# The tile loop of an attention and expert kernel, rewritten with fourfold k weights and later routing tables

## The chip, the cores and the metric

The kernel runs on one core of a Trainium2 chip. The metric is the device time of one execution in microseconds; the median of 3 runs stands for a kernel. One execution is profiled, and its records are what the rows below show.

## What is computed

The reference, cut to what matters: a row-wise attention over an image, a memory layer over the tokens, and 32 experts of which each token takes two.

```python
# x: (4, 256, 32, 32); wq, wk: (32, 256); wv: (256, 256)
q = einsum('bchw,oc->bohw', x, wq) + bq
k = einsum('bchw,oc->bohw', x, wk) + bk
v = einsum('bchw,oc->bohw', x, wv) + bv
energy = einsum('bci,bcj->bij', qf, kf).reshape(b, h, w, h, w)
attn = softmax(energy, axis=-1)
out = einsum('bchk,bhwkv->bcwv', v, attn)
x = gamma * out + x
t = to_tokens(x)                                   # 4096 tokens of 256
u = layer_norm(t)
t = t + u @ W1 + (memory @ u) @ W2 + bias          # memory: a band of 32
xt = layer_norm(t)
sel_val, sel_idx = top_k(sigmoid(xt @ expert_sel.T), 2)
h = relu(einsum('td,edh->teh', xt, keys))          # 32 experts, hidden size 64
t = t + einsum('teh,te,ehv->tv', h, w, values)     # w: sel_val at sel_idx
```

## The kernel before

The 4096 tokens are 32 tiles (NT) of 128, eight for each of the 4 images (TB). The kernel is written engine by engine: each engine has its own program in a fixed order, and semaphores tie them together. An instruction that waits holds all that stands behind it on its engine. There are two parts: the tile loop, and after it the experts, which gather the tokens sorted by expert. The change touches the first.

The tile loop is a pipeline of steps `s`. In step s each engine works on several tiles, each at another stage; the lags are named at the top: attention product S_AV = 1 step behind, turn of u S_TURN = 2, mix S_MIX = 3, memory and second norm S_NORM2 = 4, routing S_ROUTE = 5, positions S_POS = 6, sending S_SEND = 7. The stages of a tile are:

- energies (TensorE, L1112): 16 matmuls of 32 x 32 with 256 columns, in two of the array's four row groups, into `E` (two banks). VectorE takes the maximum `gmax` (L755), subtracts it (L759), ScalarE takes the exponential (L638), VectorE sums (L803) and inverts (L818), GpSimd scales by it (L496, `scale_by_sums`).
- the attention product (L1207) into `av_p`; VectorE adds the input: `t1` (L829), takes statistics with BATCH_NORM_STATS and an aggregate (L835, L838); GpSimd makes the factors of the norm in three instructions (`layer_norm_factors`, L470 to L474: add epsilon, power of -1/2, times the mean); ScalarE normalises (L617).
- `u` is turned (L1218), split into a high and a low part by ScalarE (L652) and VectorE (L845), mixed with W1 and W2 (L1147), the second half again split into `z_hi` and `z_lo` (L623, L751), and the memory band is applied (L1180). VectorE adds `t1b` and takes the statistics (L769 to L778), GpSimd makes the factors (`second_factors`), ScalarE normalises into `rows` (L657, and a second copy, L645).
- the rows are turned (L1167), the logits computed (L1188), ScalarE and VectorE make sigmoid and top two (L634, L781 to L813). TensorE counts the positions in the experts' lists (L1133, L1134); VectorE makes of them the row numbers `slot` (L774 to L795) in step s = t + S_POS; GpSimd sends both rows of each token to their slots in memory with two indirect DMAs (`scatter_rows`, L478) in step s = t + S_SEND, after `rows_complete` (L489), which waits for `slot` and for the columns that ScalarE writes (L660 to L664).

Beside these, in the first 24 steps, one v projection for the next image runs in each step (L1088, evacuated by VectorE, L734), and in the steps j = 5 and 6 of eight (QK_STEPS) a projection of q and k together over 512 columns (L1067), of which ScalarE evacuates q (L605) and VectorE k (L726).

The order of GpSimd's step is: first factors (s-2), bias (s-3), `rows_complete` and scatter r=0 (s-7), second factors (s-4), scatter r=1 (s-7), scale by sums (s). TensorE's is: energies (s), turn of the rows (s-5), v projection, memory (s-4), logits (s-5), positions (s-6), attention product (s-1), turn of u (s-2), mix (s-3). After step 31 a drain finishes the last tiles, VectorE plans the experts' lists, and the experts' part begins.

## Time and profile before

| | |
|---|---|
| median of 3 runs | 504.51 us (502.11 to 505.92) |
| profiled execution | 505.35 us |
| span of its profile, first to last instruction | 503.6 us |
| mean granted clock of TensorE | 0.908 |
| tile loop, from the first to the last `gmax` | 13.8 to 276.5 us |
| first group of the experts' weights copied | about 320 us |

In the rows times are microseconds from the span's start. A timeline row has start, length, engine, line, operation, what it writes and reads, and the number of instructions merged; in brackets the idle time of the engine before it and what ended it. "issue" is time in which the engine waited for nothing that the profile shows.

### The profile page before, as it was taken

The numbers are of one execution on the slowest core, as the hardware profiler recorded it, in microseconds if no ns is written. First come the engines' busy times: TensorE is split into PE (matmuls) and PEld (weight loads), VectorE is DVE, ScalarE is ACT, GpSimd is POOL, SyncE is SP. The second block draws the span as 40 slices with busy tenths as digits, with TensorE's granted clock in tenths as the row PEclk, the third lists the DMA queues.
The fourth block names the chain that finished last, engine by engine and source line by source line (L and its number), as shares of the span: only waits on it lengthen the run. The fifth ranks groups of instructions, "written<-read, shape, count | busy, mean of one in ns | idle before, by whom it ended". The sixth has DMA issues, their size and how long they took to land.

```text
span 503.6 us, 10097 instructions
## 1 busy us (share of the span) xinstructions
PE 403.9 (80%) x2919; PEld 307.1 (61%) x2919; DVE 375.3 (75%) x1100; ACT 229.8 (46%) x604; POOL 323.6 (64%) x481
## 2 busy tenths in 40 slices
PE   8899999999999999999999875768876484876000
PEld 4667777878778786777676753356554374765000
DVE  2888999999999999999999857566655576577100
ACT  2223454545455554554554443258665474753000
POOL 5355558888778888678888786365555555536610
PEclk9999999999999999999999987699788788888555
DMA  6998001311111111112111011476544343421096
GB/s 221 318 212 170 24 23 55 127 54 45 44 43 43 54 44 55 45 38 49 55 58 40 22 53 64 127 238 190 177 148 128 126 144 106 126 85 51 1 208 126
DMA packets 28439, 49.52 MB, mean 98 GB/s; under 512 B 6204, under 2 KB 21966, under 8 KB 27373
## 3 DMA queue, kind: packets, MB, share of 16 engines
q1 hardware_dynamic: 20512, 26.69, 20.5%
q0 software_dynamic: 7872, 22.19, 14.2%
q8 instruction: 24, 0.39, 0.3%
q14 instruction: 31, 0.25, 0.2%
HBM read 30.74 MB, written 25.73 MB: 112 GB/s over the span
## 4 chain that ended last, share of the span: by engine, by line
PE 46%; DVE 18%; issue 13%; SPq 9%; DMA 3%; another core or an unknown queue 2%; POOL 2%; DVEq 1%; ACT 1%; POOLq 0%; ACTq 0%
PE bank L1207 16%; SPq L402 7%; PE bank L1147 6%; PE E L1112 5%; PE bank L1088 4%; DVE gmax L755 2%; PE bank L1180 2%; PE bank L1067 2%; DVE gsum L803 2%; PE bank L1188 2%; PE bank L1278 2%; DMA biasb<-bias 2%; PE bank L1167 2%; PE bank L1264 1%
## 5 line engine op out<-in xcount | busy, mean ns | idle before, releaser
L578 POOL DMA_INDIRECT out<-vT,dest x80 | 79.0, 988 | 65.2 <-DVE vT L1021 44.5
L1207 PE MATMUL bank<-vT,prob 128*128 128x256 f32 x512 | 118.1, 384 | 0.2 <-POOL prob L496 0.2
L1207 PEld LDWEIGHTS bank<-vT,prob 128*128 128x128 f32 x512 | 94.9, 190 | 12.4 <-POOL prob L496 0.6
L496 POOL TENSOR_TENSOR prob<-prob,ginv 128x1024 f32<-128x1024 f32 x32 | 61.1, 1909 | 28.1 <-DVE ginv L818 25.7
L478 POOL DMA_INDIRECT slot_rows<-rows,slot x64 | 68.5, 1070 | 12.7 <-issue 12.7
L1247 PE MATMUL E<-ident,xc_or_xin 128*128 128x128 f32 x160 | 26.8, 320 | 30.0 <-DMA xc_or_xin<-slot_rows 27.0
L675 ACT ACTIVATE prob<-E 128x512 f32<-128x512 f32 x40 | 22.5, 594 | 47.8 <-PE E L1247 31.8
L1247 PEld LDWEIGHTS E<-ident,xc_or_xin 128*128 128x128 f32 x160 | 20.8, 163 | 38.0 <-DMA xc_or_xin<-slot_rows 32.5
L638 ACT ACTIVATE prob<-prob 128x1024 f32<-128x1024 f32 x32 | 33.8, 1057 | 20.9 <-DVE prob L759 20.9
L1021 DVE SCALAR_TENSOR_TENSOR vT<-bank,wgt,vT 128x256 f32<-128x256 f32 x80 | 33.2, 478 | 11.9 <-PE bank L1278 8.1
L803 DVE TENSOR_REDUCE gsum<-prob 128x32 f32<-128x1024 f32 x32 | 38.5, 1204 | 4.1 <-ACT prob L638 4.0
L682 ACT ACTIVATE vT<-xc_or_xin 128x256 f32<-128x256 f32 x80 | 41.2, 588 | 0.0
L1035 DVE COPY rows<-values_s 64x256 f32 x112 | 37.5, 335 | 3.9 <-issue 2.6
L755 DVE TENSOR_REDUCE gmax<-E 128x32 f32<-128x1024 f32 x32 | 39.0, 1220 | 1.7 <-PE E L1112 1.3
L759 DVE TENSOR_TENSOR prob<-E,gmax 128x1024 f32<-128x1024 f32 x32 | 39.2, 1225 | 1.1
L472 POOL TENSOR_TENSOR rstd<-rstd,half_neg 128x1 f32<-128x1 f32 x64 | 36.5, 571 | 5.3
L652 ACT ACTIVATE uT_hi<-bank 128x256 fp32r<-128x256 f32 x32 | 12.3, 385 | 54.2 <-PE bank L1218 54.2
L617 ACT ACTIVATE u<-t,rstd 128x256 f32<-128x256 f32 x32 | 19.2, 601 | 36.3 <-POOL rstd L474 36.1
L1112 PE MATMUL E<-k_s,q_s 32*32 32x256 f32 x1024 | 35.0, 380 | 0.4 <-DVE prob L759 0.4
L1088 PE MATMUL bank<-wv,xc_or_xin 128*128 128x256 f32 x128 | 32.6, 384 | 2.2 <-issue 1.3
L470 POOL TENSOR_SCALAR rstd<-mv 128x1 f32<-128x1 f32 x64 | 14.9, 233 | 24.4 <-DVE mv L778 19.3
L697 ACT ACTIVATE k_s<-keys_s 128x128 f32 x112 | 24.7, 298 | 11.9 <-issue 11.9
(206 smaller groups left out, 888.8 us busy)
## 6 DMA issues: line engine op xcount, KB each, us to landing
xc_or_xin<-slot_rows SPq DMA_DIRECT2D x48, 130.0 KB
xc_or_xin<-slot_rows SPq DMA_DIRECT2D x64, 65.0 KB
xt<-x_tok SPq DMA_DIRECT2D x32, 128.0 KB, 2.4
values_s<-values SPq DMA_DIRECT2D x2, 2048.0 KB, 30.5
out<-out POOLq DMA_DIRECT2D x4, 1024.0 KB, 14.3
xc_or_xin<-x_cm SPq DMA_DIRECT2D x3, 1024.0 KB, 10.4
keys_s<-keys SPq DMA_DIRECT2D x1, 2048.0 KB, 15.3
out<-vT,dest POOLq DMA_INDIRECT x80
```

The costliest lines, as they stand in the source:

```text
L478: g.indirect_dma_start(out=slots_d, out_offset=bass.IndirectOffsetOnAxis(ap=slot[:, t % RB, r:r + 1], axis=0), in_=rows[:, t % RB, r, :], ...
L496: g.tensor_tensor(prob[:, t % 2], prob[:, t % 2], ginv[:, t % 2].unsqueeze(2).to_broadcast([P, WT * KB, W]), ALU.mult).then_inc(prob_done, 1)
L578: g.indirect_dma_start(out=out, out_offset=bass.IndirectOffsetOnAxis(ap=dest[:, n % (2 * NB), k:k + 1], axis=0), in_=yb[:, n % NB, k, :], ...
L682: done = a.activation(yb[:, n % NB, k, :], xin[:, n % NB, k, 0:C], ACT.Identity, bias=xin[:, n % NB, k, MEAN:MEAN + 1], scale=xin[:, n % N ...
L755: v.tensor_reduce(gmax[:, t % 2], E[:, :].rearrange("p (a v) -> p a v", v=W), AX.X, ALU.max).then_inc(max_done, 1)
L759: v.tensor_tensor(prob[:, t % 2].rearrange("p (j w) v -> p w j v", w=WT), E[:, :].rearrange("p (w j v) -> p w j v", w=WT, v=W), gmax[:, t ...
L803: v.tensor_reduce(gsum[:, t % 2], prob[:, t % 2], AX.X, ALU.add).then_inc(sum_done, 1)
L1035: done = v.tensor_copy(into, values_s[side, bass.ds(expert[2 * k + r], 1), :].rearrange("p e n -> p (e n)"))
L1088: mm = m.matmul(v_bank(b, j)[:, 0:C], x, w, start=(i == 0), stop=(i == len(terms) - 1))
L1112: mm = m.matmul(E[g * H:(g + 1) * H, cols], q_s[at, b % 2, tb, w, :], k_s[at, b % 2, g].rearrange("p j v -> p (j v)"), start=True, stop=True)
L1207: mm = m.matmul(av_p, pr[:, j, :], vT[:, b % 2, j, :], start=(j == 0), stop=(j == KB - 1))
L1247: mm = m.transpose(T_p[q][:, k % 2, a, :], xin[:, n % NB, k, a * P:(a + 1) * P], ident[:, :])
```

## The change

TensorE:

- the energies are spread over all four row groups. k is therefore made four times, once in each group of 32 partitions: its weights stand fourfold in `wqk`, and q is made by eight small matmuls into four column groups (`q_proj`, in step j = 2), k in four pieces of 256 columns (`k_proj`, steps j = 3 to 6). `E` takes the lower half of each of four banks; what else is in PSUM moves to their upper halves and to banks 4 to 7.
- the order of the step is now: turn of the rows (s-5), energies (s), memory (s-4), logits (s-5), attention product (s-1), positions (s-6), q or k projection, mix (s-3), v projection, turn of u (s-2). The v projection waits for the `t1` sum of the same step, since both are in bank 7.

VectorE:

- the statistics go. The sums `t1` and `t2` are scalar_tensor_tensor instructions with an accumulated output (`first_sum`, `second_sum`); ScalarE takes the sum of squares (`squared`: a Square with accumulated output and a tiny activation that scales it and adds epsilon). GpSimd's factors are two instructions, the fourth one of the second norm is gone.
- the routing tables come a step later: `hot` and `hotb` in step t + S_POS, positions read, `picked` and `slot` in step t + S_SEND, all behind the subtraction of the maximum.
- k is evacuated by ScalarE (`k_evac`).

GpSimd: in steps below 31 both scatters stand behind one another, ahead of the second factors, and `scale_by_sums` is last. ScalarE: new order, below.

The diff, cut to its core:

```diff
-QK_STEPS = (5, 6)
+Q_STEP, K_STEPS = 2, (3, 4, 5, 6)
...
+        X = ps("X", [P, 2048])
+        bank = [X[:, i * 512:(i + 1) * 512] for i in range(4)] + [ps(f"bank{i}", [P, 512])[:, :] for i in range(4, 8)]
+
+        E = X.rearrange("p (w c) -> p w c", w=WT)[:, :, 0:KB * W]
+        hz_p = bank[4]
         t2_p = bank[5][:, 0:C].rearrange("p (a n) -> p a n", a=CH)
-        lg_p = bank[6][:, 0:NE]
-        pos_p = bank[5][:, C:C + NE]
-
-        first_qk_p = [E[:, 0:512], bank[7]]
-        v_banks = [2, 3, 4, 5, 6, 7]
-        LAST_QK = 5
-        BEFORE_E, BEFORE_MAX, BEFORE_SUM, BEFORE_E1 = 2, 2, 4, 6
-        cnt_p = bank[3][:, 0:NE]
-        sched_p = bank[2][0:4, 0:P]
-
-        T_p = [E[:, q * 512:(q + 1) * 512].rearrange("p (k a n) -> p k a n", k=2, a=CH) for q in range(2)]
-
-        H_two = [bank[2 + b][:, :].rearrange("p (w k n) -> p w k n", w=GROUP // 2, k=2) for b in range(2)]
-        H_half = [bank[2 + b][:, :].rearrange("p (k n) -> p k n", k=GROUP) for b in range(2)]
-        Y_p = [[bank[i + side][:, :].rearrange("p (k n) -> p k n", k=GROUP // 2) for side in range(2)] for i in (6, 4)]
+        lg_p = bank[5][:, C + NE:C + 2 * NE]
+        uT_p = bank[6][:, 0:C].rearrange("p (a n) -> p a n", a=CH)
+        qk_p = bank[6][:, C:2 * C]
+        av_p = bank[7][:, 0:C]
+        v_p = bank[7][:, C:2 * C]
+
+        first_k_p, first_q_p = [bank[4], bank[5]], bank[6][:, 0:TB * H]
+        first_v_p = [bank[i][:, C:2 * C] for i in (7, 4, 5, 6)]
+        BEFORE_E, BEFORE_MAX, BEFORE_SUM, BEFORE_E1 = 1, 1, 3, 5
...
                 for t in tiles(s, S_SEND):
                     rows_complete(t)
                     scatter_rows(t, 0)
+                    if s < NT - 1:
+                        scatter_rows(t, 1)
                 for t in tiles(s, S_NORM2):
                     second_factors(t)
+                scale_by_sums(s)
                 if s == NT - 1:
-                    scale_by_sums(s)
-                for t in tiles(s, S_SEND):
-                    scatter_rows(t, 1)
-                if s < NT - 1:
-                    scale_by_sums(s)
+                    scatter_rows(s - S_SEND, 1)
                 if s == 0:
...
+            def k_evac(b, u):
+                act.wait_ge(k_mm, k_made(b - 1) + u + 1)
+                after(act, e_mm, TB * (b - 1))
+                vs = W // len(K_STEPS)
+                a.activation(k_s[:, b % 2, :, :, u * vs:(u + 1) * vs], qk_p.rearrange("p (v j g) -> p g j v", g=WT, j=KB),
+                             ACT.Identity, bias=bqk[:, 0:1]).then_inc(k_out, 1)
...
+            def squared(x, mv_t, rstd_t, t, x_done, rstd_done, mv_done, ve_done):
+
+                act.wait_ge(x_done, t + 1)
+                after(act, ve_done, t)
+                a.activation(squares[:, :], x, ACT.Square, bias=mv_t[:, 0:1], scale=-float(C),
+                             accum_out=mv_t[:, 1:2]).then_inc(mv_done, 1)
+                act.wait_ge(mv_done, t + 1)
+                after(act, rstd_done, t - 1)
+                a.activation(rstd_t[:, 0:1], mv_t[:, 1:2], ACT.Identity, bias=eps_col[:, 0:1], scale=1.0 / C ** 3).then_inc(ve_done, 1)
...
+            for s in range(NT):
+                for t in tiles(s, S_MIX):
+                    turned(t)
+                for t in tiles(s, S_ROUTE):
+                    second_turned(t)
+                    logits_exp(t)
+                for t in tiles(s, S_TURN):
+                    first_norm(t)
+                for t in tiles(s, S_ROUTE):
+                    second_copy(t)
+                act.wait_ge(centred, s + 1)
+                a.activation(prob[:, s % 2], prob[:, s % 2], ACT.Exp).then_inc(exp_done, 1)
+                for t in tiles(s, S_POS):
+                    columns_written(t)
                 for t in tiles(s, S_NORM2):
-                    act.wait_ge(hz_mm, t + 1)
-                    a.activation(z_hi[:, t % 3], z_at(t), ACT.Copy).then_inc(z_hi_done, 1)
-                for t in tiles(s, S_ROUTE):
-                    act.wait_ge(u2T_mm, t + 1)
-                    after(act, lg_mm, t - 1)
-                    a.activation(u2T[:, t % 2], u2T_at(t), ACT.Copy).then_inc(u2T_out, 1)
-                for t in tiles(s, S_TURN):
-                    if s < NT:
-                        first_norm(t)
-                for t in tiles(s, S_ROUTE):
-                    act.wait_ge(lg_mm, t + 1)
-                    after(act, ex1_done, t - 1)
-                    a.activation(ex[:, t % 2], lg_p, ACT.Exp, scale=-1.0).then_inc(ex_done, 1)
-                t = tile(s, 0)
-                if t is not None:
-                    act.wait_ge(centred, t + 1)
-                    a.activation(prob[:, t % 2], prob[:, t % 2], ACT.Exp).then_inc(exp_done, 1)
+                    second_squares(t)
                 if s == 0:
                     act.wait_ge(ld_wmix, 48)
                     a.activation(w12_hi[:, :, :, :], w12_as, ACT.Copy).then_inc(w_hi_done, 1)
                     act.wait_ge(const_done, 1)
                     a.activation(band_r[:, :], band[:, :], ACT.Copy).then_inc(band_done, 1)
+                work = proj_work(s)
+                if work and work[1] == Q_STEP:
+                    q_evac(work[0], qk_p)
+                elif work and work[1] in K_STEPS:
+                    k_evac(work[0], K_STEPS.index(work[1]))
+                for t in tiles(s, S_NORM2):
+                    second_norm(t)
+                for t in tiles(s, S_MIX):
+                    z_high(t)
+                for t in tiles(s, S_AV):
+                    first_squares(t)
...
+            def first_sum(t):
+                dve.wait_ge(av_mm, t + 1)
+                dve.wait_ge(ld_xt[t % 4], 16 * (t // 4 + 1))
+                after(dve, t1b_done, t - 2)
+                after(dve, u1_done, t - 2)
+                after(dve, nmr1_done, t - 1)
+                v.scalar_tensor_tensor(out=t1[:, t % 3], in0=av_p, scalar=1.0, in1=xt[:, t % 4], op0=ALU.mult, op1=ALU.add,
+                                       accum_out=mv1[:, t % 2, 0:1]).then_inc(t1_done, 1)
...
+                for t in tiles(s, S_SEND):
+                    place(t)
+                for t in tiles(s, S_POS):
+                    chosen(t)
+                for t in tiles(s, S_SEND):
+                    entry_rows(t)
+                for t in tiles(s, S_POS):
+                    both_chosen(t)
                 for t in tiles(s, S_NORM2):
-                    dve.wait_ge(h_mm, t + 1)
-                    dve.wait_ge(t1b_done, t + 1)
-                    v.tensor_tensor(t2[:, t], h_at(t), t1b[:, t % 2], ALU.add).then_inc(t2_done, 1)
-                    dve.wait_ge(t2_done, t + 1)
-                    v.bn_stats(bn2[:, t % 2], t2[:, t]).then_inc(bn2_done, 1)
-                for t in tiles(s, S_POS):
-                    dve.wait_ge(pos_mm, t + 1)
-                    v.tensor_tensor(spot[:, t % 2], pos_p, ebase[:, :], ALU.add).then_inc(spot_done, 1)
-                for t in tiles(s, S_NORM2):
-                    dve.wait_ge(bn2_done, t + 1)
-                    after(dve, cols_done, t - 3)
-                    v.bn_aggr(mv2[:, t % 4], bn2[:, t % 2]).then_inc(mv2_done, 1)
+                    second_sum(t)
+                for t in tiles(s, S_MIX):
+                    turned_low(t)
+                for t in tiles(s, S_SEND):
+                    rows_of_slots(t)
...
+            def k_proj(b, u):
+                per = HW // len(K_STEPS)
+                for a in range(CH):
+                    mm = m.matmul(qk_p, wqk[:, a, 0:4 * QK], xc[:, b % 2, a, u * per:(u + 1) * per],
+                                  start=(a == 0), stop=(a == CH - 1))
+                mm.then_inc(k_mm, 1)
+
+            def q_proj(b, dst):
+
+                for a in range(CH):
+                    tokens = xc[:, b % 2, a, :].rearrange("p (t w h) -> p w t h", w=WT, h=H)
+                    for c in range(WT):
+                        mm = m.matmul(dst[c * QK:(c + 1) * QK, :], wqk[:, a, 4 * QK:5 * QK], tokens[:, c],
+                                      start=(a == 0), stop=(a == CH - 1))
+                mm.then_inc(q_mm, 1)
...
-                for w in range(WT // 2):
+                after(pe, spot_done, t - S_SEND)
+                pe.wait_ge(q_out, b + 1)
+                pe.wait_ge(k_out, k_made(b))
+                for c in range(WT):
                     for g in range(WT):
-                        for r in range(2):
-                            at = slice((2 * r + 1) * QK, (2 * r + 2) * QK)
-                            cols = slice((r * 2 + w) * KB * W, (r * 2 + w + 1) * KB * W)
-                            mm = m.matmul(E[g * H:(g + 1) * H, cols], q_s[at, b % 2, tb, w, :],
-                                          k_s[at, b % 2, g].rearrange("p j v -> p (j v)"), start=True, stop=True)
+                        at = slice(c * QK, (c + 1) * QK)
+                        mm = m.matmul(E[g * H:(g + 1) * H, c, :], q_s[at, b % 2, tb, :],
+                                      k_s[at, b % 2, g].rearrange("p j v -> p (j v)"), start=True, stop=True)
                 mm.then_inc(e_mm, 1)
...
+            for s in range(NT):
+                for t in tiles(s, S_ROUTE):
+                    second_turn(t)
+                if s > 1:
                     energies(s)
                 if s == S_MIX:
 
                     pe.wait_ge(v_out, KB)
                     for _ in range(FILL_WARM):
-                        m.matmul(bank[5][:, :], warm[:, 0:P], warm[:, :], start=True, stop=True)
+                        m.matmul(bank[4], warm[:, 0:P], warm[:, :], start=True, stop=True)
+                for t in tiles(s, S_NORM2):
+                    memory(t)
+                for t in tiles(s, S_ROUTE):
+                    logits(t)
+                for t in tiles(s, S_AV):
+                    attend(t)
+                for t in tiles(s, S_POS):
+                    positions(t)
+                work = proj_work(s)
+                if work and work[1] in (Q_STEP,) + K_STEPS:
+                    b, j = work
+
+                    after(pe, uT_lo_done, s - S_TURN)
+                    if j == Q_STEP:
+                        q_proj(b, qk_p)
+                    else:
+                        pe.wait_ge(q_out, b + 1)
+                        pe.wait_ge(k_out, k_made(b - 1) + K_STEPS.index(j))
+                        k_proj(b, K_STEPS.index(j))
+                for t in tiles(s, S_MIX):
+                    mix(t)
+                if work:
+
+                    after(pe, t1_done, s)
+                    if s == 0:
+                        pe.wait_ge(v_out, KB)
+                    v_proj(work[0], work[1], v_p)
+                for t in tiles(s, S_TURN):
+                    if work and work[1] == Q_STEP:
+                        pe.wait_ge(q_out, work[0] + 1)
+                    elif work and work[1] in K_STEPS:
+                        pe.wait_ge(k_out, k_made(work[0] - 1) + K_STEPS.index(work[1]) + 1)
+                    turn(t)
```

## Rows read from the trace of the kernel before

**Rows 1.** Timeline of VectorE: the starts of `gmax` in three steps
```profile
60.59 1.23 DVE L755 TENSOR_REDUCE gmax<-E 128x32 f32<-128x1024 f32 x1 [0.28 <-PE E L1112]
...
70.87 1.22 DVE L755 TENSOR_REDUCE gmax<-E 128x32 f32<-128x1024 f32 x1 [0.17 <-PE E L1112]
...
276.46 1.22 DVE L755 TENSOR_REDUCE gmax<-E 128x32 f32<-128x1024 f32 x1
```

**Rows 2.** Timeline of TensorE: one plain step of the second image
```profile
164.73 1.09 PE L1112 MATMUL E<-k_s,q_s 32*32 32x256 f32 x32
165.76 0.44 PE L1167 MATMUL bank<-ident,rows 128*128 128x128 f32 x2
166.03 1.03 PE L1088 MATMUL bank<-wv,xc_or_xin 128*128 128x256 f32 x4
...
167.79 3.70 PE L1207 MATMUL bank<-vT,prob 128*128 128x256 f32 x16
171.33 0.38 PE L1218 MATMUL bank<-ident,u 128*128 128x128 f32 x2
...
173.04 1.09 PE L1112 MATMUL E<-k_s,q_s 32*32 32x256 f32 x32
```

**Rows 3.** Busy time by stretch: engines (instructions), granted clock, DMA share, GB/s
```profile
219.00:276.00 57.00, 54.44 (x492) 41.43 (x476) 54.84 (x162) 28.98 (x78) 49.35 (x78) 1.00 0.17 50
276.00:310.00 34.00, 24.91 (x132) 19.88 (x132) 23.26 (x88) 13.93 (x44) 25.99 (x46) 0.93 0.10 37
```
The columns are: stretch, its length, and the busy time of PE, PEld, DVE, ACT and POOL.

**Rows 4.** Timeline of VectorE in the same plain step
```profile
165.93 1.23 DVE L755 TENSOR_REDUCE gmax<-E 128x32 f32<-128x1024 f32 x1
...
168.33 0.41 DVE L769 TENSOR_TENSOR t<-bank,t1b 128x256 f32<-128x256 f32 x1
...
169.13 0.17 DVE L774 TENSOR_TENSOR spot<-bank,lbase 128x32 f32<-128x32 f32 x1
169.25 0.18 DVE L778 BATCH_NORM_AGGREGATE mv<-bn 128x2 f32<-128x6 f32 x1
...
169.99 0.22 DVE L795 TENSOR_REDUCE slot<-picked 128x2 int32<-128x64 f32 x1
...
172.55 0.47 DVE L734 SCALAR_TENSOR_TENSOR vT<-bank,gam,gbv 128x256 f32<-128x256 f32 x1
172.93 0.42 DVE L835 BATCH_NORM_STATS2 bn<-t 128x6 f32<-128x256 f32 x1
```

**Rows 5.** Timeline of TensorE, cut at 173.1 to 173.2: energies in flight
```profile
173.04 0.45 PE L1112 MATMUL E<-k_s,q_s 32*32 32x256 f32 x8
```

**Rows 6.** Timeline of all engines: factors on GpSimd, norm on ScalarE
```profile
167.13 0.27 POOL L474 TENSOR_SCALAR rstd<-mv,rstd 128x1 f32<-128x1 f32 x1
...
167.43 0.60 ACT L617 ACTIVATE u<-t,rstd 128x256 f32<-128x256 f32 x1 [0.81 <-POOL rstd L474]
```

**Rows 7.** Timeline: indirect DMAs of GpSimd in the drain and after the plan
```profile
290.18 1.09 POOL L478 DMA_INDIRECT slot_rows<-rows,slot  x1 [0.17 <-issue]
291.58 0.97 POOL L478 DMA_INDIRECT slot_rows<-rows,slot  x1 [0.30 <-issue]
292.62 0.24 POOL L470 TENSOR_SCALAR rstd<-mv 128x1 f32<-128x1 f32 x1
292.94 0.57 POOL L472 TENSOR_TENSOR rstd<-rstd,half_neg 128x1 f32<-128x1 f32 x1
293.62 0.27 POOL L474 TENSOR_SCALAR rstd<-mv,rstd 128x1 f32<-128x1 f32 x1
...
321.03 0.15 DVE L994 SCALAR_TENSOR_TENSOR pad_r_i<-over_r,pad_r 128x2 int32<-128x2 f32 x1
...
321.99 1.00 POOL L565 DMA_INDIRECT slot_rows<-pad_rows,pad_r_i  x1 [3.87 <-DVE pad_r_i L994]
```

**Rows 8.** Timeline of TensorE: attention product of the last tile
```profile
287.49 3.61 PE L1207 MATMUL bank<-vT,prob 128*128 128x256 f32 x16
```

**Rows 9.** Groups by line: GpSimd's scaling (count, busy us, mean ns, idle before)
```profile
L496 POOL TENSOR_TENSOR prob<-prob,ginv 128x1024 f32<-128x1024 f32 x32 | 61.1, 1909 | 28.1 <-DVE ginv L818 25.7
```

550 lines of the change are left out of this document (255 added, 295 removed).

## Prediction, made before the changed kernel was run

> **What bounds the kernel now.** I read the starts of the reduction `gmax` (L755) first, which come once in each step of the tile loop, then one whole step on each engine, then the busy time by stretch, and last the places where GpSimd waits for VectorE. The loop runs 32 steps. From the eighth `gmax` (step 7) to the last (step 31) 205.6 us pass, 24 intervals of 8.57 us in the mean [rows 1]. In a plain step, from 165.93 on, all engines turn once in 8.31 us: TensorE from one `energies` to the next, 164.73 to 173.04 [rows 2]. Between these two its rows leave no hole worth naming: energies 1.03, transposes 0.27, v projection with memory, logits and positions 1.76, attention times v 3.54, the turn of u with the six mix matmuls 1.71. VectorE is busy for 54.8 of 57 us in the last batch and TensorE for 54.4 [rows 3]. So both are full, and a wait of one of them on anything new costs time at once. GpSimd is at 49.3 of 57 us, nearly full too [rows 3]. The two steps of each of the first three batches that hold the old q/k projection take some 2 us more (from 60.59 to 70.87 it is 10.28 [rows 1]); four of them are inside the mean.
>
> **What the change takes away.** VectorE loses two BATCH_NORM_STATS of 0.42 us in every step [rows 4], two small aggregates, and the evacuation of k. The sums come from the additions that are there anyway. TensorE: `energies` keeps its 16 matmuls (32 records), but spreads them over four row groups and not two. Before, eight records start together [rows 5], the 32 take 1.09 us from first start to last end [rows 2], so four waves about 0.22 us apart. With 16 together, two waves go: 0.43 us less, 0.66 us in all. If no more than eight go together the gain is nothing; that is the other bound. I take two waves, because in the rows one wave already holds all the tiles that the old layout has. Against that stands a q projection in one step of eight, and the k projection is spread over four steps: each 16 or 4 records, four column groups at once or full width, about 4 x 0.22 = 0.88 us by the records of the attention product (16 in 3.54 us [rows 2]). TensorE's own sum would be 8.31 - 0.43 = 7.88 us in a plain step, 8.76 us in a q or k step. VectorE's would be below 7.6 us. ScalarE gets two squares of 256 columns with an accumulator, two tiny ones behind them and the k evacuation. The trace has no accumulating ACTIVATE; the nearest row is the 0.60 us of the same width [rows 6], below it is nothing, above it the square and a dependent one, 1.2 us. ScalarE was busy only half of the time (29.0 of 57 us [rows 3]), and these sit in places where it would wait for GpSimd anyway (next part), so I take them as hidden; without that cover it would be up to 2 us a step.
>
> **A rule weighed.** In the new loop four matmuls in a row use the same row group and differ in the column group. The rows say that this overlaps: the old loop goes through the column groups outside and two row groups inside, so eight that start together hold each row group four times [rows 5]. The Trainium skill, page TensorE: Matmul & The Clock Gate, Part 3 (packing small matmuls), says that a weight load overlaps matmuls in flight only when the row group differs. By that rule 16 would run one behind another, 16 x 0.43 us or some 6.9 us against 0.66, and the kernel would come to about 690 us; the trace of before already speaks against it, and I give it 1 in 100.
>
> **What the change moves, and where it waits.** This decides it. `slot` for tile s-7 used to be computed in step s-1, so in step s GpSimd found it ready: scatter r=0, second factors, scatter r=1, scale. Now VectorE computes it in step s (`place`, `entry_rows`, `rows_of_slots` have lag S_SEND = 7), behind gmax, the subtraction and seven others. GpSimd's `rows_complete(s-7)` stands in the same step s, and now both scatters stand before `second_factors(s-4)`. Behind the waiting instruction are queued: scatter r=0 and r=1, then the factors, then `scale_by_sums(s)`. For the factors ScalarE's `second_norm(s-4)` waits, and behind it in ScalarE's queue `z_high`. For `second_norm` TensorE's `second_turn(s-4)` waits, which is the first of step s+1, before `energies(s+1)`. And for those `gmax(s+1)` waits. That is a closed ring of one step, with no slack in it. Its length:
>
> - gmax start to the instruction behind the subtraction: 168.33 - 165.93 = 2.40 [rows 4].
> - five small table instructions (spot, seen, hot, picked, hotb), 0.12 apart as at 169.13 and 169.25: 0.60 [rows 4].
> - t2 sum with accumulator and `uT_lo`, 0.38 each as from 172.55 to 172.93: 0.76 [rows 4]. Then the slot reduction 0.22 [rows 4]. Slots are ready at 3.98.
> - VectorE's end to the start of an indirect DMA that has waited for it: L994 ends at 321.18, L565 starts at 321.99: 0.81 [rows 7]. Where GpSimd has not waited, an indirect DMA starts 0.17 behind its predecessor [rows 7]; this is the lower bound of the term, 0.2. I take 0.81, since this one waits.
> - first scatter 1.00 [rows 7], gap 0.30 and second 0.97 (at 291.58), gap 0.07 to the next: 2.34 [rows 7].
> - reciprocal root start to the end of the third factor, 292.94 to 293.89: 0.95 [rows 7]. The addition of epsilon is gone from GpSimd; it is done by ScalarE earlier.
> - to ScalarE 0.03 (167.40 to 167.43), the norm 0.60 [rows 6].
> - to TensorE 0.05 (my estimate from the hop just named), two transposes 0.27 [rows 2], energies 0.66 (two waves), to VectorE 0.04.
>
> 3.98 + 0.81 + 2.34 + 0.95 + 0.63 + 0.32 + 0.70 = 9.73 us. That is longer than TensorE's 8.76 of a k step, so the k and q steps hide in it and every step from 7 on has the same length. The neighbouring ring over `z_high`, `z_low` and gmax is shorter: it parts from this one at the start of the norm, 8.11, and needs about 0.7 for the norm and two tiny activations, 0.39 for z_high and 0.4 for z_low, 9.6. A ring over two steps (second norm, z_high, squares, uT, u2T, logits, attention product, mix, v, turn, energies) comes to about 18.4, or 9.2 a step.
>
> Sum: 24 intervals of 9.73 are 233.5 us, against 205.6: **+27.9 us**. Before step 7 no scatter exists. There the two old q/k steps win about 1.5 us each (10.28 [rows 1] against 8.76), and the four before them, short now, lose about as much in sum, since the new v projection waits in each step for the t1 sum (exp, gsum, ginv and that sum stand ahead of it): net 0, plus or minus 2, an estimate. In the drain the attention product of the last tile starts 11.03 us after the last gmax (276.46 [rows 1] to 287.49 [rows 8]). Now it stands behind z_low, which stands behind `turned_low` and one more `slots` on VectorE, and z_high comes at 8.8: about 14.5, of which I take 3 us as lost (0 to 4). The experts' part is the same code; hT and the banks only change their place: 0. The profiled execution took 505.35 us (0.8 above the median of the runs): 505.35 + 27.9 + 3 = 536.3, and by the median 535.4. I say **536 us**.
>
> **Rivals.**
>
> 1. *The ring doesn't close, TensorE bounds (faster).* GpSimd would have its slots in time, as VectorE has spare time now. For it: the busy sums of all engines fall below 8.31. Against it: `rows_of_slots(s-7)` can't come before the subtraction of step s in VectorE's order, and gmax(s) itself waits for energies(s). Time: step 7 at 7.9, sixteen steps in two batches of 3 x 7.88 + 5 x 8.76 = 67.4 each, seven steps of the last batch at 7.4 (GpSimd: two scatters, scale 1.91 [rows 9], factors 1.9, bias 0.7 and gaps): 194.6, so 11.0 less: **494 us**. It decides once the ring is below 8.45 us a step (205.6 less the 3 of the drain, over 24), so 1.3 us shorter than I sum it. Chance 0.13.
> 2. *The scatter starts as if it hadn't waited* (0.2 and not 0.81): ring 9.12, 24 x 9.12 = 218.9, +13.3 +3: **522 us**. It lies in my forecast's own spread and holds 0.18 of its chance.
> 3. *Energies stay at four waves:* ring 10.16, 243.8, +38.2 +3: **547 us**. Chance 0.09.
> 4. *TensorE's clock falls.* Busy 54.4 of 57 us, the granted clock is 1.00; in the drain, at 24.9 of 34, it is 0.93 [rows 3], between the two levels of 2.4 and 1.2 GHz. In the last batch TensorE would work about 7.2 of 9.73 us, as thin as the drain. At 0.93 the 0.93 us of TensorE in the ring grow by less than 0.1, eight steps: under 1 us. At the lower level throughout, 14.4 us a step, eight steps: +37, about **573 us**. Chance 0.05 for anything over 550.
> 5. *A mixture near the time of now* (the ring closes but several terms overlap, 8.4 to 8.6 us a step): 505 us, chance 0.04.
>
> **Numbers.** My forecast with the spread of term four (522 to 536, and to 543 should the tiny activations delay the norm) has 0.68, 0.50 of it near 536. Two microseconds of the early steps and the drain's 0 to 4 lie on both sides: 516 to 552 holds the forecast, rival 2 and rival 3, together 0.77 and a bit of rivals 4 and 5, so 8 in 10. What stays out are the 494 and the 573. Over 1% is what a measurement here can tell. Faster by over 1%: 0.13; within 1%: 0.04; slower: 0.83.
>
> **What would show it.** In the changed kernel's profile gmax starts 9.7 us apart from step 8 on, alike in plain and k steps; the wait of GpSimd's first scatter for the slot reduction is over 1 us in each step; ScalarE waits for the factors before the second norm, and TensorE before the second transposes, for ScalarE. VectorE is busy for some 75%. If energies take 1.1 us, rival 3 holds. If gmax starts 7.9 and 8.8 us apart and TensorE has no holes, my ring is wrong, and most likely at the place of the slots. Wrong in size it would be if the term of 0.81 belongs to that one DMA only.

## The result, and the profile after

The changed kernel took 535.5 us in the median of 5 runs (531.7 to 536.5), the kernel before 504.5 in the runs beside it. The ratio is 1.060, interval 1.055 to 1.065: slower, and within 1 us of the 536 us that were forecast. The profiled execution of the changed kernel took 531.67 us. It is the fastest of its runs, 3.8 us below their median, so the comparison of the traces explains its own difference (+26.3 us of span) and not all of the 31 us between the medians.

Timeline of VectorE in the changed kernel, four starts of `gmax`, which answer to [rows 1]:

```profile
72.55 1.23 DVE L861 TENSOR_REDUCE gmax<-X 128x32 f32<-128x1024 f32 x1 [0.41 <-PE X L1146]
...
241.95 1.22 DVE L861 TENSOR_REDUCE gmax<-X 128x32 f32<-128x1024 f32 x1 [0.32 <-PE X L1146]
...
252.83 1.23 DVE L861 TENSOR_REDUCE gmax<-X 128x32 f32<-128x1024 f32 x1 [0.39 <-PE X L1146]
...
299.73 1.23 DVE L861 TENSOR_REDUCE gmax<-X 128x32 f32<-128x1024 f32 x1 [0.32 <-PE X L1146]
```

From step 7 to step 31 now 227.2 us pass, where it was 205.6: +21.6. Up to step 7 it is +1.7 (72.55 against 70.87), and from the last `gmax` to the end of the span 230.2 us against 227.1, +3.0. The sum is 26.3. The third part is not the drain alone. The first turn of gathered rows on TensorE, with which the experts' part begins, stands in the two timelines, before and after, at:

```profile
324.17 1.09 PE L1247 MATMUL E<-ident,xc_or_xin 128*128 128x128 f32 x8 [0.24 <-DMA xc_or_xin<-slot_rows]
...
352.00 1.04 PE L1318 MATMUL X<-ident,xc_or_xin 128*128 128x128 f32 x8
```

That is 47.7 us behind the last `gmax` before and 52.3 after: the drain and the plan cost 4.6 us, and the experts' part took 1.5 less than before.

The steps are strikingly even: 9.38 us, plain or with a k projection, 9.56 to 9.6 in three of them, and one single step of 10.88 (241.95 to 252.83).

One of these steps, timeline of all engines, cut to the rows of the ring (start, length, engine, line; in brackets the wait):

```profile
166.77 1.22 DVE L861 TENSOR_REDUCE gmax<-X 128x32 f32<-128x1024 f32 x1 [0.32 <-PE X L1146]
...
170.40 0.20 DVE L852 TENSOR_REDUCE slot<-picked 128x2 int32<-128x64 f32 x1
...
170.89 1.06 POOL L477 DMA_INDIRECT slot_rows<-rows,slot  x1 [2.41 <-DVE slot L852]
...
172.25 0.96 POOL L477 DMA_INDIRECT slot_rows<-rows,slot  x1 [0.30 <-issue]
...
173.24 0.58 POOL L471 TENSOR_TENSOR rstd<-rstd,half_neg 128x1 f32<-128x1 f32 x1
...
173.92 0.26 POOL L473 TENSOR_SCALAR rstd<-mv,rstd 128x1 f32<-128x1 f32 x1
...
174.22 0.60 ACT L661 ACTIVATE rows<-t,rstd 128x256 f32<-128x256 f32 x1 [2.87 <-POOL rstd L473]
...
174.87 0.44 PE L1195 MATMUL bank<-ident,rows 128*128 128x128 f32 x2 [0.69 <-ACT rows L661]
...
175.24 0.71 PE L1146 MATMUL X<-k_s,q_s 32*32 32x256 f32 x32
...
176.14 1.23 DVE L861 TENSOR_REDUCE gmax<-X 128x32 f32<-128x1024 f32 x1 [0.32 <-PE X L1146]
```

Read the brackets downwards: GpSimd waits 2.41 us for the slots, ScalarE 2.87 for the factors, TensorE 0.69 for the rows, VectorE 0.32 for the energies. Each of the four engines waits for the one before it, and the last wait ends in the instruction at which the first began. That is how a closed ring looks in a profile: nobody is full, everybody waits. The waits summed over the kernel say the same: 25 times, once in each step from 7 on. A row has the waiting instruction, what it waited for, us in total, times, and the longest.

```profile
POOL slot_rows L477 <- DVE slot L852: 61.7, 25, 3.4
ACT rows L661 <- POOL rstd L473: 51.3, 25, 3.1
```

Busy time by stretch (length, then PE, PEld, DVE, ACT, POOL with their instructions, granted clock, DMA share, GB/s), three stretches of the last batch, beside [rows 3]:

```profile
234.00:243.00 9.00, 7.28 (x66) 5.48 (x65) 6.41 (x21) 5.56 (x18) 5.86 (x9) 0.97 0.16 44
243.00:253.00 10.00, 10.00 (x67) 7.77 (x67) 6.10 (x22) 5.34 (x18) 5.52 (x7) 0.69 0.13 41
253.00:300.00 47.00, 41.18 (x341) 31.63 (x339) 34.35 (x106) 28.20 (x92) 31.24 (x41) 0.93 0.13 41
```

VectorE was busy for 54.8 of 57 us and is now for 34.4 of 47; the change did take work from it. But none of the engines uses what it was given. The long step lies in the second stretch: the granted clock falls to 0.69, and 67 records fill all of its 10 us, where 66 took 7.28 us in the first. The clock also falls in two later steps of this batch, to 0.82, and these two still take 9.38 us. One of them, from `gmax` to `gmax`:

```profile
262.21:271.59 9.38, 9.22 (x70) 7.12 (x69) 6.99 (x21) 5.57 (x19) 6.25 (x8) 0.82 0.14 44
```

TensorE's work grew to 9.22 us there, which the ring's 9.38 still hides.

The last tile's attention product [rows 8], timeline of TensorE:

```profile
313.86 3.75 PE L1221 MATMUL bank<-vT,prob 128*128 128x256 f32 x16
```

It starts 14.1 us after the last `gmax`, where it was 11.0.

### The profile page after: what moved, and what is told of

It reads as the page before. It is cut to its first block, busy times and chain, and to the rows that moved or that the text cites. A ratio compares the mean times of both kernels' runs of the same rounds, so it can differ in the third digit from the quotient of the medians.

```text
span 529.9 us, 10428 instructions
## 1 busy us (share of the span) xinstructions
PE 412.5 (78%) x3007; PEld 314.2 (59%) x3007; DVE 335.9 (63%) x1022; ACT 278.0 (52%) x828; POOL 296.3 (56%) x386
## 3 DMA queue, kind: packets, MB, share of 16 engines
q1 hardware_dynamic: 20512, 26.72, 19.5%
## 4 chain that ended last, share of the span: by engine, by line
issue 27%; POOL 20%; PE 17%; SPq 12%; ACT 10%; DVE 5%; DMA 2%; ACTq 1%; POOLq 0%; another core or an unknown queue 0%; DVEq 0%
POOL slot_rows L477 9%; SPq L402 8%; POOL rstd L471 5%; PE bank L1221 5%; POOL t1b L486 3%; ACT squares L621 3%; SPq L399 3%; PE bank L1183 2%; POOL rstd L473 2%; DMA biasb<-bias 2%; ACT rstd L625 1%; PE bank L1115 1%; ACT rows L663 1%; ACT z_hi L641 1%; PE bank L1349 1%
## 5 line engine op out<-in xcount | busy, mean ns | idle before, releaser
L1221 PE MATMUL bank<-vT,prob 128*128 128x256 f32 x512 | 123.3, 396 | 0.7 <-DVE vT L790 0.7
L1318 PE MATMUL X<-ident,xc_or_xin 128*128 128x128 f32 x160 | 26.3, 316 | 34.1 <-DMA xc_or_xin<-slot_rows 29.2
L734 ACT ACTIVATE prob<-X 128x512 f32<-128x512 f32 x40 | 22.3, 592 | 50.4 <-PE X L1318 34.9
L661 ACT ACTIVATE rows<-t,rstd 128x256 f32<-128x256 f32 x32 | 19.2, 599 | 51.5 <-POOL rstd L473 51.3
L861 DVE TENSOR_REDUCE gmax<-X 128x32 f32<-128x1024 f32 x32 | 39.2, 1224 | 10.3 <-PE X L1146 10.3
L1318 PEld LDWEIGHTS X<-ident,xc_or_xin 128*128 128x128 f32 x160 | 20.8, 161 | 41.3 <-DMA xc_or_xin<-slot_rows 33.4
L865 DVE TENSOR_TENSOR prob<-X,gmax 128x1024 f32<-128x1024 f32 x32 | 39.2, 1224 | 1.1
L790 DVE SCALAR_TENSOR_TENSOR vT<-bank,gam,gbv 128x256 f32<-128x256 f32 x32 | 15.0, 479 | 32.1 <-PE bank L1115 31.6
L621 ACT ACTIVATE squares<-t,mv 128x256 f32<-128x256 f32 x64 | 31.7, 496 | 2.6 <-DVE t L813 2.5
L1115 PEld LDWEIGHTS bank<-wv,xc_or_xin 128*128 128x128 f32 x128 | 23.5, 189 | 10.5 <-DVE t L813 4.1
## 6 DMA issues: line engine op xcount, KB each, us to landing
out<-out POOLq DMA_DIRECT2D x4, 1024.0 KB, 14.5
keys_s<-keys SPq DMA_DIRECT2D x1, 2048.0 KB, 14.5
```

Source lines behind the costliest of these rows:

```text
L621: a.activation(squares[:, :], x, ACT.Square, bias=mv_t[:, 0:1], scale=-float(C), accum_out=mv_t[:, 1:2]).then_inc(mv_done, 1)
L861: v.tensor_reduce(gmax[:, s % 2].rearrange("p (w j) -> p w j", w=WT), E.rearrange("p w (j v) -> p w j v", v=W), AX.X, ALU.max).then_inc(ma ...
L865: v.tensor_tensor(prob[:, s % 2].rearrange("p (j w) v -> p w j v", w=WT), E.rearrange("p w (j v) -> p w j v", v=W), gmax[:, s % 2].rearran ...
L1115: mm = m.matmul(dst, x, w, start=(i == 0), stop=(i == len(terms) - 1))
L1221: mm = m.matmul(av_p, pr[:, j, :], vT[:, b % 2, j, :], start=(j == 0), stop=(j == KB - 1))
L1318: mm = m.transpose(T_p[q][:, k % 2, a, :], xin[:, n % NB, k, a * P:(a + 1) * P], ident[:, :])
```

## Experiments

The theory: a ring of one step over gmax, slots, scatters, factors, second norm, rows' turn and energies sets the step, and it exists only because GpSimd waits in step s for slots that VectorE makes in step s. The rivals: TensorE or another engine bounds; the new order of GpSimd costs by itself; the row groups of the energies cost. The runs were made on three occasions. The kernel before took 508.7 us beside the first one's four (sending later, the slots earlier and later, the factors first) and 471 beside all others, so each is compared with the kernel before of its own occasion. The chip alone doesn't account for the two levels: both were measured under the same chip number, and where they come from is not known.

**Without the wait: send one step later.** GpSimd sends tile s-8 in step s; its slots were made a step ago. All else stays.

```diff
-                for t in tiles(s, S_SEND):
-                    rows_complete(t)
-                    scatter_rows(t, 0)
-                    if s < NT - 1:
-                        scatter_rows(t, 1)
+                if s > S_SEND:
+                    rows_complete(s - S_SEND - 1)
+                    scatter_rows(s - S_SEND - 1, 0)
+                    scatter_rows(s - S_SEND - 1, 1)
...
                 if s == NT - 1:
+                    rows_complete(s - S_SEND)
+                    scatter_rows(s - S_SEND, 0)
                     scatter_rows(s - S_SEND, 1)
```

> The changed kernel with one edit: in the tile loop GpSimd sends the rows of tile s-8 and not s-7, so that the row numbers were ready a step before. Ring theory (GpSimd's wait for the slot reduction holds factors, norm, turn and energies of the next step): the wait of 2.4 us a step goes, gmax starts 7.9 to 8.2 us apart in plain steps and 8.8 to 9.0 in q and k steps, against 9.38; from step 7 to 31 about 197 us against 227; in all 503 to 508 us. Rival, the added work on ScalarE (squares, accumulator reads, tiny activations) bounds the loop: gmax stays at 9.2 us apart or more, in all 525 us or more. Rival, TensorE with its new order bounds it: 8.8 us in all steps, 517 us.

Measured: 0.995 of the kernel before (0.991 to 0.998). The loss is gone. GpSimd's timeline (first scatter of one step), VectorE's (last `gmax`) and busy time by stretch in the last batch:

```profile
158.86 1.06 POOL L477 DMA_INDIRECT slot_rows<-rows,slot  x1 [0.16 <-issue]
```

```profile
271.37 1.22 DVE L862 TENSOR_REDUCE gmax<-X 128x32 f32<-128x1024 f32 x1 [0.36 <-PE X L1147]
```

```profile
219.00:271.00 52.00, 50.63 (x467) 39.49 (x466) 46.50 (x147) 38.99 (x123) 42.19 (x54) 1.00 0.16 53
```

With `gmax` of step 7 at 72.55 as in the changed kernel, 198.8 us pass to step 31, instead of 227.2. The scatter no longer waits for the slots. TensorE is busy for 50.6 of 52 us: it is full again, and the steps have three lengths again (8.10 plain, 8.7 to 9.2 with q or k, 7.6 in the last batch). This is what rival 1 of the prediction would have looked like: 194.6 us were worked out for it there, 198.8 came. A second run on another chip gave 0.995 again (0.992 to 0.999).

**The ring made shorter and longer.** The slot reduction moved ahead of the t2 sum and `uT_lo`, and in another kernel behind the sum of the exponentials. The diff is that of the first.

```diff
+                for t in tiles(s, S_SEND):
+                    rows_of_slots(t)
                 for t in tiles(s, S_NORM2):
                     second_sum(t)
                 for t in tiles(s, S_MIX):
                     turned_low(t)
-                for t in tiles(s, S_SEND):
-                    rows_of_slots(t)
```

> The changed kernel with VectorE's slot reduction moved ahead of the t2 sum and uT_lo, two instructions that take 0.68 us. Ring theory: everything behind it moves by 0.68 us: plain steps 8.70 us apart against 9.38, q and k steps limited by TensorE at 8.8 to 9.0; in all about 520 us. Rival, the slot wait is not on the path that sets the step: no change, 535 us.

> The changed kernel with VectorE's slot reduction moved behind the sum of the exponentials, 1.13 us later. Ring theory: all steps from 7 on 10.5 us apart, 24 x 1.13 = +27 us, in all about 562 us. Rival, the slot wait is not on the path: no change, 535 us.

Measured: 1.032 (1.023 to 1.041) and 1.117 (1.111 to 1.123) of the kernel before. Timeline, slot reduction and first scatter of one step, of the kernel with the earlier slots (its `gmax` at 161.89, the next at 170.63):

```profile
164.86 0.22 DVE L852 TENSOR_REDUCE slot<-picked 128x2 int32<-128x64 f32 x1
...
165.36 1.06 POOL L477 DMA_INDIRECT slot_rows<-rows,slot  x1 [1.75 <-DVE slot L852]
```

and of the one with the later slots (`gmax` at 169.99 and 180.50):

```profile
174.75 0.21 DVE L852 TENSOR_REDUCE slot<-picked 128x2 int32<-128x64 f32 x1
...
175.25 1.06 POOL L477 DMA_INDIRECT slot_rows<-rows,slot  x1 [3.54 <-DVE slot L852]
```

The slots are ready 3.19 and 4.97 us after the start of `gmax`, where it was 3.83, and the steps are 8.74 and 10.51 us, where it was 9.38: the shift of one small instruction (0.64 down, 1.14 up) goes whole into every plain step. A shift downwards stops paying in the k and q steps, which took 8.9 to 9.2 and 9.6. The medians, 524.8 and 568.2, lie 5 and 6 us above what was expected; 4 us of this is the slower occasion (508.7 and not 504.5 for the kernel before). Ten steps of the kernel with the later slots took 10.7 to 11.8, and all but the first of these overlap a stretch at a lower granted clock.

**GpSimd's order alone, in the kernel before.** Both scatters ahead of the second factors, slots early as ever.

```diff
                     rows_complete(t)
                     scatter_rows(t, 0)
+                for t in tiles(s, S_SEND):
+                    if s < NT - 1:
+                        scatter_rows(t, 1)
                 for t in tiles(s, S_NORM2):
                     second_factors(t)
+                scale_by_sums(s)
                 if s == NT - 1:
-                    scale_by_sums(s)
-                for t in tiles(s, S_SEND):
-                    scatter_rows(t, 1)
-                if s < NT - 1:
-                    scale_by_sums(s)
+                    scatter_rows(s - S_SEND, 1)
```

> The kernel before with only GpSimd's new order: both scatters ahead of the second factors, scale last. The slots are still made a step before, so GpSimd doesn't wait for them. Theory 'what costs is the wait for slots made in the same step': no change, 503 to 507 us, steps at 8.3 to 8.6. Rival 'the order alone costs, as the second factors now stand behind 2.3 us of scatters and no longer behind 1.3': the second norm comes 1.3 us later in each step, and where it bounds, up to 25 times 1.3, 535 us.

Measured: 1.003 (0.999 to 1.008). VectorE's timeline, steps 7 and 31:

```profile
70.86 1.23 DVE L755 TENSOR_REDUCE gmax<-E 128x32 f32<-128x1024 f32 x1 [0.17 <-PE E L1112]
...
276.39 1.22 DVE L755 TENSOR_REDUCE gmax<-E 128x32 f32<-128x1024 f32 x1
```

205.5 us, as in [rows 1]. In the kernel before, the order alone costs nothing.

**Factors ahead of the scatters, a miss.** If the scatters cost 2.3 us inside the ring, the factors could go before them.

```diff
+                for t in tiles(s, S_NORM2):
+                    second_factors(t)
                 for t in tiles(s, S_SEND):
                     rows_complete(t)
                     scatter_rows(t, 0)
                     if s < NT - 1:
                         scatter_rows(t, 1)
-                for t in tiles(s, S_NORM2):
-                    second_factors(t)
                 scale_by_sums(s)
```

> The changed kernel with GpSimd's second factors ahead of the wait for the row numbers; both scatters still behind that wait and ahead of the scaling. Ring theory: the one-step ring over the second norm is cut (factors ready 5.6 us after gmax, not 7.4), but the scaling now comes at 8.1 us after gmax, and over the next first factors, first norm, exp, gsum, t1 sum and v projection a ring of two steps of about 17.7 us closes: 8.6 to 8.9 us a step, in all about 518 us. Rival, only the scaling's lateness mattered: no change, 535 us. Rival, ScalarE's work: 525 us or more.

Measured: 1.068 (1.063 to 1.073), not better but worse than the change itself. The timeline of one step shows another ring, in which neither `gmax` nor a slot has a part:

```profile
168.76 1.92 POOL L495 TENSOR_TENSOR prob<-prob,ginv 128x1024 f32<-128x1024 f32 x1
...
170.62 0.57 POOL L471 TENSOR_TENSOR rstd<-rstd,half_neg 128x1 f32<-128x1 f32 x1
...
171.59 0.60 ACT L614 ACTIVATE u<-t,rstd 128x256 f32<-128x256 f32 x1 [1.85 <-POOL rstd L473]
172.10 0.59 ACT L654 ACTIVATE rows<-t,rstd 128x256 f32<-128x256 f32 x1
172.59 1.04 ACT L683 ACTIVATE prob<-prob 128x1024 f32<-128x1024 f32 x1
...
174.34 0.29 ACT L625 ACTIVATE rstd<-mv,eps_col 128x1 f32<-128x1 f32 x1
...
174.72 0.55 POOL L471 TENSOR_TENSOR rstd<-rstd,half_neg 128x1 f32<-128x1 f32 x1 [2.47 <-ACT rstd L625]
...
176.06 1.06 POOL L477 DMA_INDIRECT slot_rows<-rows,slot  x1 [0.43 <-issue]
...
177.42 0.97 POOL L477 DMA_INDIRECT slot_rows<-rows,slot  x1 [0.30 <-issue]
...
178.41 1.93 POOL L495 TENSOR_TENSOR prob<-prob,ginv 128x1024 f32<-128x1024 f32 x1
```

Scale 1.9, first factors 0.9, on ScalarE first norm, copy, exponential and squares 3.0, second factors 1.0, a gap of 0.4, two scatters 2.3: 9.65 us from scale to scale. In the changed kernel the scatters lie beside ScalarE's 3 us; here they come behind them. The next run tests this reading: the same order, but the tile of step s-8, so that no slot is waited for.

```diff
                 for t in tiles(s, S_NORM2):
                     second_factors(t)
-                for t in tiles(s, S_SEND):
-                    rows_complete(t)
-                    scatter_rows(t, 0)
-                    if s < NT - 1:
-                        scatter_rows(t, 1)
+                if s > S_SEND:
+                    rows_complete(s - S_SEND - 1)
+                    scatter_rows(s - S_SEND - 1, 0)
+                    scatter_rows(s - S_SEND - 1, 1)
                 scale_by_sums(s)
                 if s == NT - 1:
+                    rows_complete(s - S_SEND)
+                    scatter_rows(s - S_SEND, 0)
                     scatter_rows(s - S_SEND, 1)
```

> The changed kernel with GpSimd's second factors ahead of the scatters, as in the run that came out slower than the changed kernel, and the scatters sending the tile one step later, so that no slot of the same step is waited for. Theory from that run's trace: there the bound was another ring, without slots or maximum: scale ends, first factors 0.9, then on ScalarE the first norm, its copy, the exponential and the squares 3.0, second factors 0.9, gap 0.4, both scatters 2.3, scale 1.9, in sum 9.65 us a step. It doesn't hold a slot, so sending later changes nothing: steps at 9.6, about 540 us. Rival 'the slots were the bound there too, by way of the late maximum': the steps fall to 8.1 to 9.1 as in the run that only sends later, about 505 to 510 us.

Measured: 1.072 (1.065 to 1.079), as slow as with the fresh slots. VectorE's timeline, steps 7 and 31, 230.4 us apart, 9.60 a step in the mean:

```profile
72.31 1.22 DVE L862 TENSOR_REDUCE gmax<-X 128x32 f32<-128x1024 f32 x1 [0.42 <-PE X L1147]
...
302.71 1.23 DVE L862 TENSOR_REDUCE gmax<-X 128x32 f32<-128x1024 f32 x1 [0.39 <-PE X L1147]
```

The single `gmax` intervals are uneven here, 8.1 to 11.7 us. What is even is GpSimd's scale, 9.65 to 9.75 apart from 98.8 us on, but for one of 10.00, and 9.64 to 9.67 in the run before. Two of its starts in this run's timeline of GpSimd:

```profile
186.19 1.93 POOL L495 TENSOR_TENSOR prob<-prob,ginv 128x1024 f32<-128x1024 f32 x1
...
195.84 1.93 POOL L495 TENSOR_TENSOR prob<-prob,ginv 128x1024 f32<-128x1024 f32 x1
```

So this ring runs through the scale and holds neither the slots nor `gmax`. Taken together: sending later is worth 28 us of loop where the scatters stand ahead of the factors, and 1 us where they stand behind them (231.5 against 230.4).

**The clock.** The changed kernel, with one multiplication more on TensorE in each of the last eight steps, where no v projection is left (its result is read by nobody).

```diff
                     v_proj(work[0], work[1], v_p)
+                else:
+                    after(pe, t1_done, s)
+                    for a in range(CH):
+                        m.matmul(v_p, xc[:, 1, a, 0:P], wv[:, a, :], start=(a == 0), stop=(a == CH - 1))
```

> The changed kernel, but in the last eight steps, where no v projection is left, TensorE multiplies once more into the v bank (4 records, about 1 us), to be nearer to its activity in the steps before. The results of these matmuls are read by nobody. In the changed kernel's profile one step of the last batch took 10.88 us and not 9.38, and it began with the granted clock falling (242.5 to 249.3). Theory 'the thin TensorE of the last batch lets the clock fall, and only there it costs': no stretch at the low clock between steps 24 and 31, all steps of the last batch at 9.38, the loop's end 1.5 us earlier in a profile with that fall, so about 530 to 535 and within 0.5% of the changed kernel. Theory 'the ring sets the step, and a TensorE with 1 us more work has it to spare': the filler costs nothing, since TensorE waits there for ScalarE's rows. Rival 'TensorE is in fact at its limit in the last batch': the steps grow by up to 1 us each, 540 us.

Measured: 1.061 (1.053 to 1.069), the changed kernel's ratio. Busy time in its last batch:

```profile
242.00:298.00 56.00, 50.60 (x430) 39.09 (x430) 40.26 (x127) 33.80 (x108) 37.18 (x48) 1.00 0.13 42
```

The granted clock is 1.00 throughout, all its steps in this stretch are 9.38, and none is long. Beside it, the kernel of the next run, without the filler, has two long steps there (10.8 and 10.9) with granted clocks of 0.68 and 0.69. So in these profiles, one of each kernel, the clock falls in the last batch without the added work and not with it. A step at 0.68 or 0.69 takes some 1.5 us more; the two at 0.82 in the changed kernel took nothing more. The ring, not the clock, makes the 9.38. The gain of the filler is within what these runs can tell.

**Row groups.** The two loops of the energies exchanged, so that neighbouring matmuls differ in the row group.

```diff
-                for c in range(WT):
-                    for g in range(WT):
+                for g in range(WT):
+                    for c in range(WT):
```

> The changed kernel with the two inner loops of the energies exchanged: neighbouring matmuls now differ in the row group and share the column group, where they shared the row group before. My theory: up to 16 go together whatever their order, so energies stay at 0.71 us from first start to last end and the time is that of the changed kernel (within 0.5%, period 9.38). Rival, by a rule of the Trainium skill, page TensorE: Matmul & The Clock Gate, Part 3 (packing small matmuls), that a weight load overlaps matmuls in flight only when the row group differs: the order of the changed kernel would pay for it and this one not, so energies get shorter here, by 0.2 us or more in each ring: 24 times 0.2, 530 us or below.

Measured: 1.063 (1.056 to 1.070). Its timeline of TensorE:

```profile
157.89 0.71 PE L1146 MATMUL X<-k_s,q_s 32*32 32x256 f32 x32
```

0.71 us, as in the changed kernel, and steps of 9.38. Between these two orders there is no difference. The rule of the Trainium skill weighed in the prediction (page TensorE: Matmul & The Clock Gate, Part 3, packing small matmuls), that weight loads overlap only where the row group differs, doesn't describe this trace: with four neighbours in one row group and with neighbours in different ones the energies take the same 0.71 us.

**What the term of 0.81 us was.** The prediction took it from an indirect DMA with a bounds check [rows 7]; the tile loop's have none, and there the hop is 0.29. The changed kernel with such a check on the loop's scatters:

```diff
-                    in_=rows[:, t % RB, r, :], in_offset=None).then_inc(scattered[t % RB], 16)
+                    in_=rows[:, t % RB, r, :], in_offset=None,
+                    bounds_check=NE * CAP - 1, oob_is_err=False).then_inc(scattered[t % RB], 16)
```

> The changed kernel; only the indirect DMAs of the tile loop get a bounds check (all slots lie inside it, so the same rows are written), like the one DMA in the kernel before from which the prediction took 0.81 us between VectorE's end and the DMA's start. In the changed kernel's trace that hop was 0.29, and what differs in the records are register moves ahead of the DMA that has the check. Theory 'the 0.81 belongs to the bounds check': the hop rises from 0.29 to 0.8, the step from 9.38 to 9.9 at least; where the second scatter needs its own moves, to 10.4. Loop 7 to 31 by 12 to 24 us longer, 544 to 558 us on a chip where the changed kernel takes 531. Rival 'the 0.81 came from elsewhere, such as the first use of that list or a longer wait there': hop and step stay, time within 0.5% of the changed kernel.

Measured: 1.093 (1.085 to 1.101), steps of 9.92. Its timeline:

```profile
167.62 0.21 DVE L853 TENSOR_REDUCE slot<-picked 128x2 int32<-128x64 f32 x1
...
168.64 1.06 POOL L477 DMA_INDIRECT slot_rows<-rows,slot  x1 [2.93 <-DVE slot L853]
...
170.01 0.97 POOL L477 DMA_INDIRECT slot_rows<-rows,slot  x1 [0.30 <-issue]
```

From the end at 167.83 to 168.64 it is 0.81 us, to the hundredth what [rows 7] had. The hop grows by 0.52 and the step by 0.54. The second scatter keeps its gap of 0.30, so here the check costs behind a wait and not behind another scatter. The ratio lies 0.03 above those of the filler and the exchanged loops, 1.061 and 1.063, beside a kernel before of the same 471 us: 24 times 0.54 is 13 us, and five of its steps are long (10.4 to 11.5), four of them at a granted clock of 0.68 to 0.70.

**A better one.** The kernel that sends later, with another order at the head of the drain: VectorE makes `z_lo` of tile 28 before `uT_lo` and the slots, and TensorE does the last attention product right behind the turn of the rows.

```diff
+            z_low(NT - S_NORM2)
             turned_low(NT - S_MIX)
...
                 for t in tiles(s, S_NORM2):
-                    z_low(t)
+                    if s > NT:
+                        z_low(t)
...
                     second_turn(t)
+                for t in tiles(s, S_AV):
+                    attend(t)
                 for t in tiles(s, S_NORM2):
                     memory(t)
...
                     mix(s - S_MIX)
-                for t in tiles(s, S_AV):
-                    attend(t)
```

The loop's change is that of the first experiment.

> Once more the changed kernel that sends a tile one step later, beside the run below on the same chip. By the first time it was run: 0.995 of the kernel before, steps of 8.10 in the plain ones, 9.1 in the q step, 8.7 to 8.9 in the k steps, last gmax at 271.4.

> The kernel that sends one step later, with another order at the start of the drain: VectorE makes z_lo of tile 28 before uT_lo and the slots, and TensorE takes the attention product of the last tile right behind the turn of the rows, where it waited 2.88 us for that z_lo. The loop doesn't change (last gmax at 271.4). Theory 'the drain lost its 3 us by that order': the last attention product starts some 4 us earlier, at 279 to 280 and not 283.7, and the end comes 1 to 4 us earlier: 0.987 to 0.993 of the kernel before. Rival 'the drain is bound by GpSimd's scatters and factors of the last tiles, so TensorE's order is hidden': no change against the run with the old drain (0.995).

Measured: 0.995 (0.992 to 0.999) and 0.992 (0.989 to 0.996) of the kernel before. TensorE's timeline, last attention product, of the first (its last `gmax` at 270.76):

```profile
280.37 0.58 PE L1205 MATMUL bank<-z_hi,band_r 128*128 128x256 f32 x1 [2.88 <-DVE z_lo L806]
...
284.88 4.34 PE L1222 MATMUL bank<-vT,prob 128*128 128x256 f32 x16
```

and of the second (last `gmax` at 272.93):

```profile
280.45 3.72 PE L1224 MATMUL bank<-vT,prob 128*128 128x256 f32 x16 [0.80 <-POOL prob L495]
```

It starts 7.5 us after the last `gmax` and not 14.1. Of these 6.6 us only 2.2 arrive at the experts' first turn (50.3 and 52.5 us behind the last `gmax`), so the last attention product alone doesn't hold the drain. The medians are 1.5 us apart (467.8 and 469.3) and the means of ten runs each 2.0, about three times the standard error of that difference, while the two ratios' intervals overlap. That the drain's order helps is likely, and no more. Both beat the kernel before, by less than one per cent.

## Why the prediction was right

**The ring and its terms.** The sum was made of seven terms; the step at 166.77 gives each:

| from, to | forecast | measured |
|---|---|---|
| gmax start, slots ready | 3.98 | 3.83 |
| to the scatter's start | 0.81 | 0.29 |
| two scatters, to the factors | 2.34 | 2.35 |
| factors | 0.95 | 0.94 |
| second norm, with its hop | 0.63 | 0.64 |
| to TensorE, two transposes | 0.32 | 0.42 |
| energies and hop to gmax | 0.70 | 0.90 |
| sum | 9.73 | 9.37 |

The mechanism held in every link, and the runs with shifted slots show that the links are in series. One term was mis-sized. The 0.81 was read off the only GpSimd DMA in the trace that had waited for VectorE, but that one has a bounds check, and the run with the check shows that it makes the difference. The prediction named this doubt ("if the term of 0.81 belongs to that one DMA only") and gave the other value, as its rival 2 with 9.12; the truth lay between, since the hop is 0.29 and not 0.2, the last two rows were summed 0.1 and 0.2 too short and the first 0.15 too long.

**Energies.** Two waves were forecast with 0.66 us and 0.71 came, against 1.09 before. Rival 3 (four waves) is out. So is the price of the row groups.

**The sum.** 24 steps of 9.73 were to cost 27.9 us; they cost 21.6: 24 times 9.38 less 205.6 is 19.5, the long step adds 1.5, and 0.2 each in three steps with other work. The early steps were taken as 0, give or take 2, and cost 1.7: the two old q/k steps won 2.9 us, as forecast, but the five beside them lost 5.0, and the first `gmax` came 0.4 earlier. The drain was put at 3, with the last attention product 14.5 us behind the last `gmax`, and this came at 14.1. The drain itself cost 4.6 us to the experts' first turn. In the profiles of the filler and the exchanged loops it was 51.9 and 53.8 us, against 46.8 in the kernel before with the scatters together, so 5 to 7 us. The experts' part, put at 0, gave 1.5 back, and so the two together are the 3.0.

**Right by a little luck.** Against the profile the forecast of 536.3 is 4.6 us too high (531.67), against the median of 535.5 by 0.8. The ring's error of 0.35 us a step, 8.4 in all, was made up by the early steps (1.7), the long step and the three with other work (2.1), and by the 4 us that the other executions took over the profiled one. Where these 4 us lie isn't known; more long steps at a low clock are a candidate, since the profile with the exchanged loops had two of them, each worth 1.5, but no trace of those executions exists.

**Rivals.** TensorE at its limit (494) needed the ring open, and in the kernel that sends later it comes about: the prediction's condition was a mean step below 8.45, and it is 8.28 there. The whole kernel isn't near 494 even so, since the early steps and the drain take back most of the 6.8 us that the loop gains. Rival 4, the clock, was there in kind and small: one step, 1.5 us, where "under 1 us" was forecast for the mild case. ScalarE's squares were put at nothing. ScalarE's timeline in the changed kernel:

```profile
170.44 0.49 ACT L621 ACTIVATE squares<-t,mv 128x256 f32<-128x256 f32 x1
...
170.83 0.19 ACT L621 ACTIVATION_READ_ACCUMULATOR squares<-t,mv 128x1 f32 x1
...
171.05 0.29 ACT L625 ACTIVATE rstd<-mv,eps_col 128x1 f32<-128x1 f32 x1
```

They end at 171.34, and then ScalarE waits 2.87 us for GpSimd, so they cost nothing in this ring. With the factors first they are in a ring, and there they cost.

**What the working missed.** All rings that were laid out pass the energies and `gmax`. The run with the factors first was expected at 518 and came at 543 (of this 4 us by the slower occasion), since GpSimd's scale, both factors, ScalarE and the scatters close a ring of their own. It has no part in the changed kernel, where the scatters lie beside ScalarE's work. The ring over two steps was summed too long: 18.4 us, or 9.2 a step, but in the kernel that sends later, which still has every link that the prediction listed for it, all 24 steps are shorter and plain ones take 8.10. As the one-step ring was longer in either case, the forecast didn't suffer. Still open: in 11 of the last 24 steps of the kernel with the factors first `gmax` starts 1.2 to 1.7 us after the modelled end of the energies although VectorE is free, where it is 0.2 in the changed kernel. It lies outside the ring, and its cause was not found.

## What to carry to other kernels

In a kernel of many engines in fixed order, moving the making of a value one step later, past its consumer, makes the consumer wait. Moving the consumer one step later too took the wait away here. If it doesn't move, look for the closed path through the waiting instruction's queue back to the producer, and sum it with the hops between the engines. If the sum is above the fullest engine's step, expect it as the new step, whatever work the change took away. Lay out every ring that passes the moved instruction, also those without the value that was moved, and take the price of an instruction only from one of the same form.
